# In a decoder layer with a selective scan, half of the scan's B·u products move from VectorE to ScalarE and GpSimd

## The chip, the cores and the metric

One core of a Trainium2 chip runs the whole kernel in one launch. The metric is the device time in microseconds, as the median of several runs. The engines are TensorE (PE), VectorE (DVE), ScalarE (ACT), GpSimd (POOL) and SyncE (SP). Each works through a row of instructions of its own, in order, and waits on semaphores for the others.

## The reference, cut to what matters

One decoder layer on 16 x 128 tokens of width 128: a selective state space block with a mixture of 4 experts, an attention, and a second mixture of 8 experts. The part that the change touches is the recurrence, per channel and for 16 states:

```python
def step(h, inps):
    x_t, d_t, B_t, C_t = inps
    bar_A = jnp.exp(jnp.minimum(d_t[:, :, None] * A, 2.0))
    bar_B = jnp.clip(d_t[:, :, None] * B_t[:, None, :], -2.0, 2.0)
    h = jnp.clip(bar_A * h + bar_B * x_t[:, :, None], -100.0, 100.0)
    y = jnp.sum(h * C_t[:, None, :], axis=-1) + x_t * D_param
    return (h, y)
```

The mixtures, the attention, the layer norms and their inputs all follow from y and are computed as before.

## The kernel before, in words

Channels lie on the 128 partitions, tokens along the free axis. The 16 sequences form four groups of four, 512 tokens each. A *unit* is one state of one group: k // 16 is the group, k % 16 the state, 64 units in all. For each unit

- ScalarE computes the decay a = exp(A·delta) in SBUF (`decay`, in batches of four, four to seven units ahead),
- TensorE broadcasts the row of B into a PSUM bank (`send_B`, banks 0 and 3 in turn) and the row of C into bank 1 (`send_C`),
- VectorE multiplies the B bank in place with u = delta·x (`drive`, L489), runs the scan h = a·h + drive (`scan`, L502), and multiplies h with C into hc (`read_out`, L537),
- GpSimd adds hc to the running output yD (`add_state`, L1072).

What sets the order is a loop over *slots* k that each engine's code runs through for itself; there is no other scheduler. In slot k VectorE issues scan(k), drive(k+1), read_out(k-1), then `around(k)`, the small work that is due in that slot. GpSimd's slot k is add_state(k-1) and then its share of the other work: in slots 5, 21 and 37 it splits rows into three bf16 parts, in others it adds a bias (L1020), forms delta (L1090), u (L1094) or a bound (L1098), or an inverse root. TensorE's slot k is send_B(k+2), its other work, send_C(k+1). The other work is the preparation of the next group, the first mixture of the group before and the attention of the one before that, all placed by slot number; from group 1 on it fills most of each engine's row. h is a ring of 3 units, hc of 3, a of 8. After slot 63 the tail begins: the last group's mixture and attention, the routing and the eight experts.

Every semaphore wait stands in the engine's own row, so all that is behind the waiting instruction waits too. `dve_done` counts VectorE's instructions, and `at[...]` holds the count of one of them.

Once for each group VectorE also bounds |h| (a scan of z, L468, both inputs in SBUF); where the bound is too large a slow clipped path runs, which these inputs do not take.

Of the kernel before, what the change touches and what calls it, by code (L numbers as in the profile page):

```python
# [5 lines left out]
ALU = mybir.AluOpType  # L6
# [143 lines left out]
def decoder_layer(nc, x, ctx, A_log, D_param, Wd, bd, WB, bB, WC, bC, Wr, br, up_w, up_b, down_w,  # L150
                  down_b, ln_w, ln_b, Wq, bq, Wk, bk, Wv, bv, wg, fc1_w, fc1_b, fc2_w, fc2_b,
                  ln_gamma, ln_beta, out):
    with ExitStack() as st:
# [39 lines left out]
            "p (e t d) -> p e t d", e=E2, t=FT)  # L193
        xe_early = sb("xe_early", [P, E2, ROW])
        xe_tok = sb("xe_tok", [P, 2, LT, ROW])
        xe_flat = w2[:].rearrange("p e t d -> p (e t d)")
        xeT = xe_flat[:, 0:2 * LATE].rearrange("p (b n) -> p b n", b=2)
        xeT_early = xe_flat[:, 2 * LATE:2 * LATE + LATE0]
# [113 lines left out]
        rows_ps, rows_done = sem("rows_ps"), sem("rows_done")  # L312
        bmax_ps, absx_done, amax_done = sem("bmax_ps"), sem("absx_done"), sem("amax_done")
        worst_ps = sem("worst_ps")
        a_done, B_ps, C_ps, y_started, summed = sem("a_done"), sem("B_ps"), sem("C_ps"), sem("y_started"), sem("summed")
        fcT_ps, fcT_done = sem("fcT_ps"), sem("fcT_done")
        ctxT_ps, ctxT_done = sem("ctxT_ps"), sem("ctxT_done")
# [45 lines left out]
            return ATT_BANK if g < G - 2 else C_BANK  # L363

        def drive_of(k):
            return bank[B_BANKS[k % 2]][:, 0:width(k // NS)]

        def state_of(k):
            return h[:, k % H_RING, 0:width(k // NS)]
# [12 lines left out]
        def _(v):  # L382
# [108 lines left out]

            def scan(k, clipped):

                v.wait_ge(dve_done, at["b", k])
                v.wait_ge(a_done, k + 1)
                if k >= H_RING:
                    v.wait_ge(dve_done, at["hc", k - H_RING])
                if clipped:
                    scan_clipped(k)
                    ins = v.tensor_scalar(state_of(k), state_of(k), CLIP_H, -CLIP_H, ALU.min, ALU.max)  # L500
                else:
                    ins = v.tensor_tensor_scan(state_of(k), decay_of(k).rearrange("p j n -> p (j n)"),  # L502
                                               drive_of(k), 0.0, ALU.mult, ALU.add)
                do(ins)
                at["h", k] = n[0]
# [283 lines left out]
            def slot(k, clipped=False):  # L789
                if 0 <= k < UNITS:  # L790
                    scan(k, clipped)
                if 0 <= k + 1 < UNITS and k >= 0:
                    drive(k + 1)
                if 1 <= k <= UNITS:
                    read_out(k - 1)
                around(k)
# [180 lines left out]
        def _(pool):  # L977
# [86 lines left out]
            def add_state(k):  # L1064
# [6 lines left out]
                pool.wait_ge(dve_done, at["hc", k])  # L1071
                pool.tensor_tensor(grp(yD, g), grp(yD, g), read_of(k), ALU.add).then_inc(summed, 1)  # L1072

            for k in range(FIRST_SLOT, LAST_SLOT + 1):
                if 0 <= k - 1 < UNITS:
                    add_state(k - 1)
                if k == PRE0:
                    inverse_root(quads(0), 0, 0)
                if k == PRE0 + 1:
                    inverse_root(slice(GT, TILES), 1, 0)  # L1080
                if (g := pre_at(k, 5)) is not None and g:
                    split_rows(g)
                if (g := pre_at(k, 13)) is not None:
                    pool.wait_ge(normed[0], g + 1)
                    pool.wait_ge(ld_affine, 16 * N_AFFINE)
                    add_bias(quads(g), 1)
                if (g := pre_at(k, 7)) is not None:
                    pool.wait_ge(sp_ln, g + 1)
                    pool.wait_ge(relu_done, g + 1)
                    pool.tensor_tensor(quad(delta, g), quad(delta, g), z1[:], ALU.add).then_inc(delta_done, 1)  # L1090
                if (g := pre_at(k, 8)) is not None:
                    pool.wait_ge(delta_done, g + 1)
                    pool.wait_ge(xT_done[0], g + 1)
                    pool.tensor_tensor(quad(u, g), quad(delta, g), quad(xT, g), ALU.mult).then_inc(u_done, 1)  # L1094
                if (g := pre_at(k, 11)) is not None:
                    pool.wait_ge(dve_done, at["boundmax", g])
                    pool.wait_ge(absx_done, g + 1)
                    pool.tensor_tensor(z2[:], z2[:], absx[:], ALU.mult).then_inc(w_done, 1)  # L1098
                if (g := att_at(k, 0)) is not None:
                    inverse_root(gsl(g), g, 1)  # L1100
                if (g := att_at(k, 3)) is not None:
                    inverse_root(gsl(g), g, 2)
                if (g := att_at(k, 5)) is not None:

                    pool.wait_ge(normed[2], g + 1)
                    add_bias(gsl(g), 4)
                if (g := att_at(k, 13)) is not None:
                    inverse_root(gsl(g), g, 3)
                if (g := att_at(k, 14)) is not None:

                    pool.wait_ge(normed[3], g + 1)
                    pool.tensor_copy(acc[:, gsl(g), :], xn[:, gsl(g), :]).then_inc(acc_done, 1)
                    pool.wait_ge(biased[4], g + 1)
                    add_bias(gsl(g), 3)
                for g, i in firsts_at(k):
                    if i == 0:
                        pool.wait_ge(zeroed, 16 * (QN + 2 * PG))
                    if i == START[G - 1]:
                        pool.wait_ge(scattered, 16 * 2 * START[G - 1])
                        pool.wait_ge(ld_early, 16)  # L1120
                    if i == counted(g).start:
                        pool.wait_ge(dve_done, at["pos", 0, g])
                    dispatch(0, i)
                    if i == TILES - 1:
                        pool.wait_ge(dve_done, at["pos", 1, g])
                        for second_of in tiles_of(g):
                            dispatch(1, second_of)
                if k in SECONDS_PARTS:
                    pool.wait_ge(dve_done, at["seconds"])
                    for i in SECONDS_PARTS[k]:  # L1130
                        dispatch(1, i)
# [23 lines left out]
        def _(act):  # L1155
# [40 lines left out]
            def silu(g, i):  # L1196
# [3 lines left out]
                if f == 0 and m >= 2:  # L1200
                    act.wait_ge(dn_ps, downs((m - 2) // E1, (m - 2) % E1 + 1))
                act.activation(hid[:, m % 2, f, 0:width(g)], bank[UP_BANKS[f % 2]][:, 0:width(g)], ACT.Silu,  # L1202
                               bias=cols[:, C_UPB + i:C_UPB + i + 1]).then_inc(hid_done, 1)

            for k in range(FIRST_SLOT, LAST_SLOT + 1):

                if (g := pre_at(k, 1)) is not None:
                    normalize(0, g, quads(g), xn, x_tok)
                if (g := att_at(k, 1)) is not None:
# [144 lines left out]
        def _(pe):  # L1354
# [19 lines left out]

            def send_B(k):
                if k >= 2:
                    pe.wait_ge(dve_done, at["h", k - 2])
                broadcast_row(B_BANKS[k % 2], k % NS, k // NS, B_ps)

            def send_C(k):  # L1380
# [191 lines left out]
            for k in range(FIRST_SLOT, LAST_SLOT + 1):  # L1572
                if k == 0:
                    send_B(0)
                    send_B(1)
                    send_C(0)
                if 0 <= k and k + 2 < UNITS:
                    send_B(k + 2)
                around(k)
                if k >= 0:  # L1580
                    next_up(k + 1)
                if 0 <= k and k + 1 < UNITS:
                    send_C(k + 1)
# [120 lines left out]
```

## Time and profile before

| | us |
|---|---|
| median of 3 runs | 481.47 (481.04 to 482.59) |
| profiled execution, its time | 482.02 |
| profiled execution, its span | 480.2 |
| TensorE busy | 344.7 (72%) |
| VectorE busy | 292.0 (61%) |
| ScalarE busy | 263.0 (55%) |
| GpSimd busy | 230.6 (48%) |
| granted TensorE clock, mean | 0.885 |

The shares are means over the whole span. The scan of the 64 units runs from 31 to 252 us, and the remaining 228 us hold the tail; the engines' shares differ between the two. A group of instructions in the profile has a line, an engine, an operation, its count, its busy time, the mean of one, and the idle time of the engine ahead of it with what ended it. Instructions of one engine overlap a little in the trace, so the pitch of their starts is shorter than their duration.

### The profile page before, as it was taken

What the parts mean: (1) busy time and instruction counts of PE and PEld (TensorE: products, weight loads), DVE (VectorE), ACT (ScalarE), POOL (GpSimd) and SP (SyncE); (2) the same over time, 40 slices, a digit from 0 to 9 for tenths busy, and PEclk for the clock granted to TensorE, in tenths of its full rate; (3) what the DMA queues carried; (4) which work ended last, traced back from release to release, by engine and by line L of the source; (5) the groups of instructions that cost most, each with busy time, mean ns of one, the idle gap of its engine ahead of it and who ended that gap; (6) DMA issues with size and microseconds to landing.
All of it is one profiled execution on the core that took longest, in us unless ns stands there. A gap on an engine that the chain in (4) does not pass through costs nothing. (4 is left out here: it accounts for less than half of the span.)

```text
span 480.2 us, 5947 instructions
## 1 busy us (share of the span) xinstructions
PE 344.7 (72%) x1749; PEld 233.6 (49%) x1749; DVE 292.0 (61%) x840; ACT 263.0 (55%) x465; POOL 230.6 (48%) x275
## 2 busy tenths in 40 slices
PE   1427557769896899978999688661537789999460
PEld 0203333346464565645667455561327757767360
DVE  3478988956999799999974245357136012222055
ACT  3554645668887797868537675413224474554021
POOL 4425755543545665464541422716844435455434
PEclk9999965879999899999899988975558899999966
DMA  6999400000000000000000000200120221210243
GB/s 123 290 233 333 124 1 1 0 0 1 1 1 0 2 1 1 1 2 0 1 1 2 0 0 9 81 1 23 50 61 28 77 67 49 76 53 14 78 120 88
DMA packets 29472, 23.94 MB, mean 50 GB/s; under 512 B 5448, under 2 KB 23943, under 8 KB 29440
## 3 DMA queue, kind: packets, MB, share of 16 engines
q1 hardware_dynamic: 27048, 19.50, 14.8%
q0 software_dynamic: 2304, 4.04, 2.5%
q8 instruction: 14, 0.23, 0.2%
q14 instruction: 18, 0.15, 0.1%
q10 hardware_dynamic: 88, 0.03, 0.0%
HBM read 13.73 MB, written 10.52 MB: 51 GB/s over the span
## 5 line engine op out<-in xcount | busy, mean ns | idle before, releaser
L1072 POOL TENSOR_TENSOR yD<-yD,hc 128x512 f32<-128x512 f32 x64 | 84.4, 1318 | 103.5 <-DVE hc L537 97.9
L1398 PE MATMUL bank<-yD,w 128*128 128x512 f32 x128 | 71.9, 645 | 17.1 <-ACT hid L1202 16.2
L502 DVE TENSOR_TENSOR_SCAN h<-a,bank 128x512 f32<-128x512 f32 x64 | 77.8, 1216 | 1.4 <-DVE bank L489 0.5
L1407 PE MATMUL bank<-w,hid 128*128 128x128 f32 x512 | 74.6, 293 | 0.0
L1407 PEld LDWEIGHTS bank<-w,hid 128*128 128x128 f32 x512 | 68.6, 205 | 9.4 <-issue 6.1
L1389 PE MATMUL bank<-rows,selid 99*128 99x512 bf16 x128 | 47.5, 457 | 25.5 <-DVE hc L537 23.4
L1135 POOL DMA_INDIRECT y_rows<-yslot,dest x40 | 39.1, 977 | 37.6 <-DVE yslot L865 22.1
L1202 ACT ACTIVATE hid<-bank,cols 128x512 f32<-128x512 f32 x64 | 43.4, 683 | 18.0 <-PE bank L1398 11.9
L489 DVE TENSOR_TENSOR bank<-bank,u 128x512 f32<-128x512 f32 x64 | 43.8, 684 | 14.5 <-PE bank L1389 14.2
L1060 POOL DMA_INDIRECT slots_in<-xrow,posu x32 | 32.3, 1010 | 32.7 <-DVE locs L684 14.7
L1389 PEld LDWEIGHTS bank<-rows,selid 99*128 99x128 bf16 x128 | 12.8, 106 | 67.4 <-DVE hc L537 47.0
L537 DVE TENSOR_TENSOR hc<-h,bank 128x512 f32<-128x512 f32 x64 | 43.3, 677 | 0.9 <-PE bank L1389 0.9
L1181 ACT ACTIVATE a<-delta,A_sb 128x508 f32<-128x508 f32 x64 | 40.5, 707 | 0.1
L865 DVE TENSOR_TENSOR yslot<-bank,w 128x128 f32<-128x128 f32 x32 | 9.2, 292 | 47.8 <-PE bank L1643 46.6
L593 DVE SCALAR_TENSOR_TENSOR acc<-bank,gate,acc 128x128 f32<-128x128 f32 x64 | 18.0, 344 | 29.5 <-PE bank L1407 29.4
L1338 ACT ACTIVATE hid<-bank,cols 128x512 f32<-128x512 f32 x32 | 22.0, 687 | 24.4 <-PE bank L1643 17.0
L1187 ACT ACTIVATE xrow<-x_tok,nmr,rstd 128x128 f32<-128x128 f32 x48 | 19.7, 482 | 23.2 <-POOL nmr L1037 23.2
L1372 PE MATMUL bank<-ident,xrow 128*128 128x128 f32 x48 | 9.5, 331 | 31.7 <-ACT xrow L1187 31.6
L1398 PEld LDWEIGHTS bank<-yD,w 128*128 128x128 f32 x128 | 20.8, 204 | 20.7 <-ACT hid L1202 18.1
L1643 PE MATMUL bank<-fc,hid 128*128 128x128 f32 x256 | 30.1, 275 | 0.7 <-DVE yslot L865 0.7
L1643 PEld LDWEIGHTS bank<-fc,hid 128*128 128x128 f32 x256 | 29.4, 192 | 1.8 <-issue 1.8
L1631 PE MATMUL bank<-w,fc1T 128*128 128x512 f32 x64 | 29.2, 596 | 1.5 <-ACT w L1320 1.5
(235 smaller groups left out, 586.4 us busy)
## 6 DMA issues: line engine op xcount, KB each, us to landing
slots_in<-yslot SPq DMA_DIRECT2D x10, 258.0 KB, 6.3
xe_tok<-slots_in SPq DMA_DIRECT2D x8, 258.0 KB
y_rows<-yslot SPq DMA_DIRECT2D x8, 256.0 KB, 5.2
x_tok<-in_x_dram SPq DMA_DIRECT2D x4, 256.0 KB, 3.9
w<-in_L_attn_up_w_dram SPq DMA_DIRECT2D x1, 1024.0 KB
yD<-y_rows SPq DMA_DIRECT2D x4, 256.0 KB, 4.4
xT<-y_rows SPq DMA_DIRECT2D x4, 256.0 KB, 5.7
out_dram<-acc SPq DMA_DIRECT2D x4, 256.0 KB, 2.3
```

Source lines behind the costliest of these rows:

```text
L489: do(v.tensor_tensor(drive_of(k), drive_of(k), grp(u, g), ALU.mult))
L502: ins = v.tensor_tensor_scan(state_of(k), decay_of(k).rearrange("p j n -> p (j n)"), drive_of(k), 0.0, ALU.mult, ALU.add)
L537: do(v.tensor_tensor(read_of(k), state_of(k), bank[C_BANK][:, 0:width(k // NS)], ALU.mult))
L1060: pool.indirect_dma_start(slots_in[:], bass.IndirectOffsetOnAxis(ap=posu[:, r, i:i + 1], axis=0), xrow[:, i, :], None, bounds_check=SLOTS - 1,
L1072: pool.tensor_tensor(grp(yD, g), grp(yD, g), read_of(k), ALU.add).then_inc(summed, 1)
L1135: pool.indirect_dma_start(y_rows[:], bass.IndirectOffsetOnAxis(ap=to, axis=0), yslot[:, half, j * P:(j + 1) * P], None, bounds_check=2 * T ...
L1181: act.activation(decay_of(k)[:, :, 1:P], tiles3(grp(delta, g))[:, :, 1:P], ACT.Exp, scale=A_sb[:, s:s + 1]).then_inc(a_done, 1)
L1202: act.activation(hid[:, m % 2, f, 0:width(g)], bank[UP_BANKS[f % 2]][:, 0:width(g)], ACT.Silu, bias=cols[:, C_UPB + i:C_UPB + i + 1]).then ...
L1389: pe.matmul(bank[b][:, 0:width(g)], selid[:, row:row + 1].to_broadcast([3 * NROW, P]), rows[:, p % 2, at_col:at_col + width(g)], start=Tru ...
L1398: pe.matmul(bank[UP_BANKS[f % 2]][:, 0:width(g)], w1[:, e, f * P:(f + 1) * P], grp(yD, g), start=True, stop=True).then_inc(up_ps, 1)
L1407: ins = pe.matmul(bank[DOWN_BANK][:, j * P:(j + 1) * P], hid[:, m % 2, f, j * P:(j + 1) * P], w2[:, e, f, :], start=(f == 0), stop=(f == F ...
L1643: ins = pe.matmul(bank[4 + t % 2][:, 0:P], hid2[:, e % 2, f, j * P:(j + 1) * P], fc2[:, e, f, :], start=(f == 0), stop=(f == FT - 1))
```

## The change

Even units keep what they had. For odd units ScalarE copies the broadcast B from PSUM bank 3 into `bu`, a ring of two units in SBUF (`copy_B`), and GpSimd multiplies it in place with u (`drive` on GpSimd). The scan of an odd unit reads `bu` in place of the bank. `bu` lies in the memory of `xe_tok`, which is loaded only in the tail. TensorE sends two B rows at the start of each even slot, and the odd one waits for ScalarE's copy instead of the scan.

```diff
@@ drive_of
-            return bank[B_BANKS[k % 2]][:, 0:width(k // NS)]
+            if k % 2:
+                return bu[:, k // 2 % 2, 0:width(k // NS)]
+            return bank[B_BANKS[0]][:, 0:width(k // NS)]
@@ VectorE, scan
-                v.wait_ge(dve_done, at["b", k])
+                if k % 2:
+                    v.wait_ge(bu_done, k // 2 + 1)
+                else:
+                    v.wait_ge(dve_done, at["b", k])
@@ VectorE, slot
-                if 0 <= k + 1 < UNITS and k >= 0:
+                if 0 <= k + 1 < UNITS and k >= 0 and k % 2:
                     drive(k + 1)
@@ GpSimd
+            def drive(k):
+
+                pool.wait_ge(b_copied, k // 2 + 1)
+                pool.wait_ge(u_done, pre_of(k // NS) + 1)
+                pool.tensor_tensor(drive_of(k), drive_of(k), grp(u, k // NS), ALU.mult).then_inc(bu_done, 1)
+
             for k in range(FIRST_SLOT, LAST_SLOT + 1):
+                if 0 <= k < UNITS and k % 2 == 0:
+                    drive(k + 1)
                 if 0 <= k - 1 < UNITS:
                     add_state(k - 1)
@@ ScalarE
+            def copy_B(k):
+
+                act.wait_ge(B_ps, k + 1)
+                if k >= 4:
+                    act.wait_ge(dve_done, at["h", k - 4])
+                act.activation(drive_of(k), bank[B_BANKS[1]][:, 0:width(k // NS)], ACT.Copy).then_inc(b_copied, 1)
+
             for k in range(FIRST_SLOT, LAST_SLOT + 1):
 
+                if k == 0:
+                    copy_B(1)
+                if k % 2 and 0 <= k and k + 2 < UNITS:
+                    copy_B(k + 2)
@@ TensorE, send_B and the loop
-                    pe.wait_ge(dve_done, at["h", k - 2])
+                    if k % 2:
+                        pe.wait_ge(b_copied, k // 2)
+                    else:
+                        pe.wait_ge(dve_done, at["h", k - 2])
...
-                if 0 <= k and k + 2 < UNITS:
+                if 0 <= k and k + 2 < UNITS and k % 2 == 0:
                     send_B(k + 2)
+                    send_B(k + 3)
```

GpSimd's row, from slot 6 on, before. L1072 is the sum of a unit, L1090 and L1094 form delta and u of the next group, L1098 the bound:

```order
L1072 TENSOR_TENSOR yD<-yD,hc 128x512 x2
L1090 TENSOR_TENSOR delta<-delta,z 128x512
L1072 TENSOR_TENSOR yD<-yD,hc 128x512
L1094 TENSOR_TENSOR u<-delta,xT 128x512
L1072 TENSOR_TENSOR yD<-yD,hc 128x512 x3
L1098 TENSOR_TENSOR z<-z 128x512
L1072 TENSOR_TENSOR yD<-yD,hc 128x512 x2
```

The same place after. L1085 is the new product (`bu` is named `xe_tok` here, after its memory), L1079 the sum, L1105, L1109 and L1113 are delta, u and the bound:

```order
L1085 TENSOR_TENSOR xe_tok<-xe_tok,u 128x512
L1079 TENSOR_TENSOR yD<-yD,hc 128x512 x2
L1105 TENSOR_TENSOR delta<-delta,z 128x512
L1085 TENSOR_TENSOR xe_tok<-xe_tok,u 128x512
L1079 TENSOR_TENSOR yD<-yD,hc 128x512
L1109 TENSOR_TENSOR u<-delta,xT 128x512
L1079 TENSOR_TENSOR yD<-yD,hc 128x512
L1085 TENSOR_TENSOR xe_tok<-xe_tok,u 128x512
L1079 TENSOR_TENSOR yD<-yD,hc 128x512 x2
L1113 TENSOR_TENSOR z<-z 128x512
```

The product of the odd unit k+1 stands at the head of even slot k, behind the sum of unit k-2 and the rest of slot k-1, ahead of the sum of unit k-1.

VectorE's row at the start of the scan, slots 0 to 3, before. A scan is listed as SCALAR_TENSOR_TENSOR:

```order
L502 SCALAR_TENSOR_TENSOR h<-a,bank 128x512
L489 TENSOR_TENSOR bank<-bank,u 128x512
L502 SCALAR_TENSOR_TENSOR h<-a,bank 128x512
L489 TENSOR_TENSOR bank<-bank,u 128x512
L537 TENSOR_TENSOR hc<-h,bank 128x512
L502 SCALAR_TENSOR_TENSOR h<-a,bank 128x512
L489 TENSOR_TENSOR bank<-bank,u 128x512
L537 TENSOR_TENSOR hc<-h,bank 128x512
L502 SCALAR_TENSOR_TENSOR h<-a,bank 128x512
```

The same slots after:

```order
L509 SCALAR_TENSOR_TENSOR h<-a,bank 128x512
L509 SCALAR_TENSOR_TENSOR h<-a,xe_tok 128x512
L493 TENSOR_TENSOR bank<-bank,u 128x512
L544 TENSOR_TENSOR hc<-h,bank 128x512
L509 SCALAR_TENSOR_TENSOR h<-a,bank 128x512
L544 TENSOR_TENSOR hc<-h,bank 128x512
L509 SCALAR_TENSOR_TENSOR h<-a,xe_tok 128x512
```

Every second product is gone from VectorE's row, and every second scan reads both inputs from SBUF.

## Rows read from the trace of the kernel before

**Rows 1.** Page, costliest groups: busy us, mean ns, idle before with releaser.

```profile
L1072 POOL TENSOR_TENSOR yD<-yD,hc 128x512 f32<-128x512 f32 x64 | 84.4, 1318 | 103.5 <-DVE hc L537 97.9
...
L502 DVE TENSOR_TENSOR_SCAN h<-a,bank 128x512 f32<-128x512 f32 x64 | 77.8, 1216 | 1.4 <-DVE bank L489 0.5
...
L489 DVE TENSOR_TENSOR bank<-bank,u 128x512 f32<-128x512 f32 x64 | 43.8, 684 | 14.5 <-PE bank L1389 14.2
...
L537 DVE TENSOR_TENSOR hc<-h,bank 128x512 f32<-128x512 f32 x64 | 43.3, 677 | 0.9 <-PE bank L1389 0.9
```

**Rows 2.** Windows: stretch, length, busy us and count of each engine, PE clock, DMA.

```profile
31.00:75.00 44.00, 25.49 (x81) 12.83 (x81) 41.11 (x56) 20.27 (x33) 25.07 (x23) 0.86 0.53 157
75.00:132.00 57.00, 45.33 (x187) 25.08 (x188) 45.40 (x85) 40.87 (x59) 27.69 (x25) 0.84 0.00 1
132.00:192.00 60.00, 52.72 (x278) 34.35 (x278) 54.85 (x114) 49.66 (x74) 33.23 (x35) 0.97 0.00 1
192.00:252.00 60.00, 53.76 (x287) 34.85 (x285) 55.27 (x134) 38.16 (x66) 29.93 (x32) 0.97 0.00 1
```

**Rows 3.** Waits from 96 to 252 us: total us, times, longest.

```profile
POOL yD L1072 <- DVE hc L537: 64.6, 34, 6.0
...
DVE bank L489 <- PE bank L1389: 12.1, 12, 4.9
```

**Rows 4.** Timeline of VectorE, slots 48 and 49: start us, duration us.

```profile
194.03 0.68 DVE L537 TENSOR_TENSOR hc<-h,bank 128x512 f32<-128x512 f32 x1
194.62 1.21 DVE L502 TENSOR_TENSOR_SCAN h<-a,bank 128x512 f32<-128x512 f32 x1
195.75 0.67 DVE L489 TENSOR_TENSOR bank<-bank,u 128x512 f32<-128x512 f32 x1
196.34 0.68 DVE L537 TENSOR_TENSOR hc<-h,bank 128x512 f32<-128x512 f32 x1
```

**Rows 5.** Timeline of GpSimd at five places.

```profile
48.73 0.30 POOL L1042 CAST parts<-bcm 128x132 bf16<-128x132 f32 x1
...
121.87 2.05 POOL L1072 TENSOR_TENSOR yD<-yD,hc 128x512 f32<-128x512 f32 x1 [0.42 <-DVE hc L537]
...
177.69 1.27 POOL L1098 TENSOR_TENSOR z<-z 128x512 f32<-128x512 f32 x1
178.92 1.27 POOL L1020 TENSOR_TENSOR x_tok<-x_tok,affine 128x512 f32<-128x512 f32 x1
180.14 2.19 POOL L1072 TENSOR_TENSOR yD<-yD,hc 128x512 f32<-128x512 f32 x1
...
194.85 1.27 POOL L1072 TENSOR_TENSOR yD<-yD,hc 128x512 f32<-128x512 f32 x1 [1.63 <-DVE hc L537]
...
209.41 0.20 POOL L1037 TENSOR_TENSOR nmr<-nmr,rstd 128x4 f32<-128x4 f32 x1
```

**Rows 6.** Timeline of VectorE: two instances of the z scan, both inputs in SBUF.

```profile
121.64 1.22 DVE L468 TENSOR_TENSOR_SCAN z<-am,z 128x512 f32<-128x512 f32 x1
...
179.15 2.12 DVE L468 TENSOR_TENSOR_SCAN z<-am,z 128x512 f32<-128x512 f32 x1
```

**Rows 7.** Groups of instructions: ScalarE's copies out of PSUM.

```profile
L1172 ACT ACTIVATE xT<-bank 128x512 f32<-128x512 f32 x12 | 7.1, 595 | 19.3 <-PE bank L1372 16.8 <-issue 2.5
```

**Rows 8.** Timeline of VectorE: C products that bound some pairs, and product 24.

```profile
44.56 0.68 DVE L537 TENSOR_TENSOR hc<-h,bank 128x512 f32<-128x512 f32 x1
...
51.09 0.68 DVE L537 TENSOR_TENSOR hc<-h,bank 128x512 f32<-128x512 f32 x1
...
102.55 0.70 DVE L489 TENSOR_TENSOR bank<-bank,u 128x512 f32<-128x512 f32 x1 [4.89 <-PE bank L1389]
...
204.34 0.68 DVE L537 TENSOR_TENSOR hc<-h,bank 128x512 f32<-128x512 f32 x1
...
211.71 0.68 DVE L537 TENSOR_TENSOR hc<-h,bank 128x512 f32<-128x512 f32 x1
...
237.44 0.68 DVE L537 TENSOR_TENSOR hc<-h,bank 128x512 f32<-128x512 f32 x1
```

**Rows 9.** Timeline of ScalarE, slots 20 and 21: a batch of decays, then silu.

```profile
93.06 2.53 ACT L1181 ACTIVATE a<-delta,A_sb 128x508 f32<-128x508 f32 x4
...
97.55 1.28 ACT L1202 ACT_TABLE_LOAD   x1
98.85 1.27 ACT L1202 ACTIVATE hid<-bank,cols 128x512 f32<-128x512 f32 x2
```

More of the change, by code:

```diff
@@ L195, in decoder_layer @@
         xe_tok = sb("xe_tok", [P, 2, LT, ROW])
+        bu = xe_tok[:].rearrange("p b j n -> p (b j n)")[:, 0:2 * GW].rearrange("p (r n) -> p r n", r=2)
         xe_flat = w2[:].rearrange("p e t d -> p (e t d)")
@@ L314, in decoder_layer @@
         worst_ps = sem("worst_ps")
+        b_copied, bu_done = sem("b_copied"), sem("bu_done")
         a_done, B_ps, C_ps, y_started, summed = sem("a_done"), sem("B_ps"), sem("C_ps"), sem("y_started"), sem("summed")
```

## The prediction

> **What bounds the kernel now.** I read the page's groups first. The scan over 64 units takes four large operations a unit: VectorE's scan (1,216 ns), its product B·u (684), its product with C (677), and GpSimd's sum into yD (1,318) [rows 1]. Then the windows: VectorE is busy 41.11 of 44 us in the first group of units, 54.85 of 60 in the third, 55.27 of 60 in the fourth; in the second, 45.40 of 57, TensorE and ScalarE hold it up [rows 2]. Then the waits of 96 to 252 us: GpSimd waits 64.6 us for VectorE's C product, so it is the slack engine; VectorE waits 12.1 us for the broadcasts [rows 3]. So VectorE's in-order row sets the scan's pace, 31 to 252 us. In the timeline of a slot without other work its instructions start 0.59 us (C product to scan), 1.13 (scan to B product) and 0.59 (B product to C product) apart, 2.31 us a slot [rows 4]. What follows 252 us is not touched and starts when the scan ends.
>
> **What is removed.** 32 products leave VectorE's row, one per pair of slots (even k, odd k+1). One is worth its pitch, 0.59 us, not its 684 ns: 32 x 0.59 = 18.9 us if nothing takes their place [rows 4].
>
> **What is added on ScalarE.** 32 copies of 512 columns from PSUM; the nearest row, the same form, is 595 ns: 19 us in a row that is busy 149 of the 221 us from 31 to 252 [rows 2, 7]. No table load stands ahead of such a copy in the trace. The copy for unit k+2 stands at the head of ScalarE's slot k, more than a slot before it is needed, so I cost it at nothing where ScalarE keeps up. The cover is gone where an exponential batch and table loads stand ahead of it, in slots 5, 21 and 37; in slot 21 it ends near 100.1 us (the silu pair ahead starts at 98.85) [rows 9], counted below.
>
> **What is added on GpSimd, and where.** 32 products of 128x512. GpSimd's own two-input products and sums last 1.27 us and follow each other by 1.23 to 1.24 [rows 5]. In its row drive(k+1) stands behind add(k-2) and whatever GpSimd does in slot k-1, and ahead of add(k-1). Take time 0 as the start of the C product of unit k-2. By the rows the scan of unit k starts at 0.59, add(k-2) at 0.82 [rows 4, 5]. Without the product the C product of k-1 starts at 1.72, and VectorE wants to scan unit k+1 at 2.31. But GpSimd starts drive(k+1) at 0.82 + 1.23 = 2.05 and ends it at 3.3. This is the first stall, at least 1.0 us, because add(k-2) cannot start earlier than it does today.
>
> **The second stall.** The scan before reads decay in SBUF and drive in PSUM, and its 64 instances take 1,216 ns in the mean; the one at 194.62 took 1.21 us although a sum of GpSimd started at 194.85 [rows 1, 4, 5]. The odd scans will read both from SBUF. The trace has a scan of that form, of z: 1.22 us where it starts before GpSimd's sum, which then lasts 2.05 instead of 1.27; 2.12 us where a GpSimd sum began 0.23 us ahead of it [rows 5, 6]. They exclude each other for a whole instruction. In the new order GpSimd ends drive(k+1) and goes straight on to add(k-1), whose input has long been there, at 3.28; VectorE still needs the semaphore, about 0.2 us. So the sum goes first, until 4.55, and the scan behind it ends 1.08 us after that, as the z scan did (181.27 against 180.19) [rows 5, 6]: 5.63. The unit k product starts 0.08 before that end, the C product of unit k 0.58 later: 6.13 us a pair. Before it was 4.60 at the faster pitch, 4.82 in the first group.
>
> The Trainium skill (SBUF — State Buffer, "Who interferes with whom") says the same as a rule that speaks against this change: a VectorE instruction with two SBUF inputs contends with a GpSimd instruction that reads SBUF, with one SBUF input it does not, and whoever issues first holds the shared ports for the whole instruction. The trace agrees, 2.12 against 1.22 us. By this rule the pair takes 6.13 us; without it 5.1.
>
> **The sum, pair by pair**, each as new minus old distance between the C products of units k-2 and k; the old ones are differences of rows like those of [rows 4, 8]:
> - Bare pairs (k = 2, 4, 10, 16, 32, 36, 48): 6.13 against 4.82, 4.82, 5.86, 4.83, 5.01, 5.03 and 5.22, the longer ones holding a wait for TensorE or a small operation: +7.3 us.
> - One more GpSimd operation of the slot before stands ahead of drive: 7.36 us. k = 8, 14, 30, 46, 60 had 4.82, 5.21, 6.49, 7.02 and 5.25 (from 237.44 on) [rows 8]: +8.0. k = 12, 28, 44, where VectorE's z scan is also held: +0.9 each, 2.7. k = 40: +0.8. k = 24 and 26 together +0.5, since VectorE waited for TensorE there.
> - Five small operations split the rows ahead of drive (k = 6, 22, 38). At k = 6 they end at 49.03, 4.47 after time 0; drive, sum and scan make it 8.55 against 6.53 [rows 5, 8]: +2.0. At k = 22 ScalarE's copy ends near 100.1, product, sum and scan put the next product at 103.7 against 102.55 [rows 8, 9]: +1.15, which also swallows k = 20. k = 38: +1.7. Together 4.9.
> - The inverse root ahead of drive (k = 42, 52, 58). At k = 52 it ends at 209.61, 5.27 after time 0, and the pair takes 9.4 against 7.37 [rows 5, 8]: +2.0; the two others +0.7 each: 3.4.
> - Where VectorE has 1.6 us or more of other work in the even slot, or the first pair, both stalls hide (k = 0, 18, 34, 50, 54, 56, 62): -4.5.
>
> Together 7.3 + 8.0 + 2.7 + 0.8 + 0.5 + 4.9 + 3.4 - 4.5 = +23.1 us. Only 4.5 of the 18.9 us are gained, in the covered pairs. I give a later scan end to the total one to one: TensorE and ScalarE work off their rest from 252 us on in the order they have now. The profiled execution has a span of 480.2 and a time of 482.02 us; 482.02 + 23.1 = 505.1, and the median of the runs lies 0.55 under it: **504.6 us**.
>
> **PSUM and TensorE.** The broadcast of an odd B now waits only for ScalarE's copy and goes out a slot earlier. It is one instruction earlier in TensorE's row, ahead of the slot's other work; cost nothing, and some of VectorE's 12.1 us of waits [rows 3] go, at most the share counted above.
>
> **Rivals.**
> - *No exclusion between odd scan and sum* (the drive in PSUM was not what spared the scan). Then only the queue position counts: the pair 5.1 us, about 1.0 less in bare pairs and in those with one more operation, 20 pairs, so 505 - 20 = 485. Against: the 2.12 us row. Chance 0.1.
> - *The stalls hide, the change gains.* This needs GpSimd to be done with drive(k+1) when VectorE asks. It is so wherever VectorE is itself held long in both slots. If it were general, 18.9 less about 5 for pairs that TensorE sets (VectorE's 12.1 us of waits, part of them kept): 468. For it: GpSimd is idle 64.6 us in that stage. Against: that idle time lies before add(k-2), drive stands after it. Chance 0.05.
> - *ScalarE becomes the bound*, slower than forecast. It has 49.66 of 60 us busy from 132 to 192 [rows 2]; 8 copies make it 54.4. Each copy is now in a chain TensorE - ScalarE - GpSimd - VectorE, and silu, which feeds TensorE, is queued behind it. If eight of the places behind an exponential batch (2.53 us, and 1.28 for a table load) [rows 9] cost 1.5 us more each, 505 + 12 = 517. It decides when ScalarE's idle time in a slot is under 0.6 us. Chance 0.2, as slower slots also give it room.
> - *Nothing changes*: gains and stalls cancel, as the first rival with more cover would have it, near 481. Chance 0.03.
> - The forecast, give or take 8 us: 0.62.
>
> **Range and chances.** Low 488 (the first rival's upper edge; pairs I took as stalled may be covered), high 518 (the third). About 0.3% is what a measurement of this kernel tells from no change. Faster 0.05, same 0.03, slower 0.92.
>
> **What would show it.** In the changed trace: odd scans of 2.0 to 2.3 us, even ones 1.21; GpSimd's product at 1.27 us, followed at once by the sum; bare pairs of 6.1 us; VectorE's idle time ahead of odd scans released by GpSimd's product, 1 us or more each, some 25 to 35 us in all; copies near 600 ns; the scan's end at about 275 instead of 252 us, and the same 228 us behind it. Wrong, if odd scans take 1.2 us under a running sum, if the copy, not the product's place in the row, is what the odd scan waits for, or if TensorE's granted clock, 0.97 in the last two groups [rows 2], falls with the slower pace.

## The result and the profile after

| | before | changed |
|---|---|---|
| median us | 482.03 (4 runs, 481.04 to 484.96) | 504.03 (4 runs, 502.88 to 507.83) |
| ratio | | 1.046, 95% interval 1.0387 to 1.0533 |
| profiled execution, span us | 480.2 | 501.1 |
| last C product of the scan starts | 251.27 | 277.37 |
| granted TensorE clock, mean | 0.885 | 0.848 |

The change costs 22.0 us, 4.6%. The page's groups of the changed kernel, which answer to [rows 1]; the scans are from the groups kept apart by form. The columns are busy us, mean ns of one, and idle us before with its releaser:

```profile
L1079 POOL TENSOR_TENSOR yD<-yD,hc 128x512 f32<-128x512 f32 x64 | 83.7, 1308 | 72.6 <-DVE hc L544 69.2
L509 DVE TENSOR_TENSOR_SCAN h<-a,xe_tok 128x512 f32<-128x512 f32 x32 | 60.4, 1889 | 25.4 <-POOL xe_tok L1085 23.5
L1085 POOL TENSOR_TENSOR xe_tok<-xe_tok,u 128x512 f32<-128x512 f32 x32 | 42.0, 1311 | 13.4 <-ACT xe_tok L1225 13.1
L544 DVE TENSOR_TENSOR hc<-h,bank 128x512 f32<-128x512 f32 x64 | 42.7, 668 | 1.6 <-DVE h L509 1.0
L509 DVE TENSOR_TENSOR_SCAN h<-a,bank 128x512 f32<-128x512 f32 x32 | 38.8, 1212 | 0.5 <-DVE bank L493 0.4
```

The even scans last 1,212 ns as before, the odd ones 1,889 in the mean: 20 of the 32 lasted 2.17 to 2.29 us, most others 1.20 to 1.23. VectorE was idle 25.4 us ahead of the odd ones, 23.5 of it until GpSimd's product. 32 x (1,889 - 1,212) ns is 21.7 us in longer scans. Together that is 47 us of loss on VectorE. From 31 us to the last C product its waits for the experts' matmuls also grew, from 3.9 to 12.3 us, and the four z scans took 2.1 us more. Against this stand the removed products, 18.9 us by their pitch (43.8 us busy in [rows 1], 21.5 now), and the waits of the B product for its broadcast, 14.2 us before and 0.7 now. The balance is some 25 us, and the last C product came 26.1 us later.

The two stalls are seen in one bare pair. VectorE, slots 32 and 33 (start us, duration us):

```profile
143.68 0.67 DVE L544 TENSOR_TENSOR hc<-h,bank 128x512 f32<-128x512 f32 x1
144.27 1.21 DVE L509 TENSOR_TENSOR_SCAN h<-a,bank 128x512 f32<-128x512 f32 x1
145.40 0.66 DVE L544 TENSOR_TENSOR hc<-h,bank 128x512 f32<-128x512 f32 x1
147.02 2.29 DVE L509 TENSOR_TENSOR_SCAN h<-a,xe_tok 128x512 f32<-128x512 f32 x1 [0.97 <-POOL xe_tok L1085]
149.23 0.67 DVE L493 TENSOR_TENSOR bank<-bank,u 128x512 f32<-128x512 f32 x1
149.81 0.67 DVE L544 TENSOR_TENSOR hc<-h,bank 128x512 f32<-128x512 f32 x1
```

and GpSimd beside it:

```profile
144.49 1.27 POOL L1079 TENSOR_TENSOR yD<-yD,hc 128x512 f32<-128x512 f32 x1 [2.40 <-DVE hc L544]
145.72 1.27 POOL L1085 TENSOR_TENSOR xe_tok<-xe_tok,u 128x512 f32<-128x512 f32 x1
146.95 1.28 POOL L1079 TENSOR_TENSOR yD<-yD,hc 128x512 f32<-128x512 f32 x1
150.63 1.27 POOL L1079 TENSOR_TENSOR yD<-yD,hc 128x512 f32<-128x512 f32 x1 [2.40 <-DVE hc L544]
```

GpSimd's product cannot start before the sum of unit 30 is through (145.72) and ends at 146.99. VectorE, free since 146.06, starts its scan at 147.02, but the sum of unit 31 had started at 146.95 and holds the scan until 148.2, so that it takes 2.29 us. From C product to C product the pair is 6.13 us, where it was 5.01, or 4.60 where nothing waited.

### The profile page after: what moved, and what is told of

The parts are those of the page before. It is cut to its first block, busy times and chain, and to the rows that moved or that the text cites. A ratio compares the mean times of both kernels' runs of the same rounds, so it can differ in the third digit from the quotient of the medians.

```text
span 501.1 us, 6009 instructions
## 1 busy us (share of the span) xinstructions
PE 356.2 (71%) x1749; PEld 239.9 (48%) x1749; DVE 298.2 (60%) x808; ACT 279.2 (56%) x497; POOL 274.3 (55%) x307
## 4 chain that ended last, share of the span: by engine, by line
PE 38%; DVE 17%; issue 16%; POOL 15%; ACT 9%; DMA 3%; another core or an unknown queue 2%; DVEq 1%; SPq 0%; POOLq 0%; ACTq 0%
PE bank L1436 7%; PE bank L1673 6%; PE bank L1661 6%; PE bank L1427 5%; POOL xe_tok L1085 4%; DVE bank L493 3%; DVE hc L544 3%; POOL yD L1079 3%; PE bank L1418 2%; POOL rstd L1040 2%; POOL slots_in L1067 2%; DVE acc L600 2%; PE bank L1519 2%; DVE z L472 1%
## 5 line engine op out<-in xcount | busy, mean ns | idle before, releaser
L1079 POOL TENSOR_TENSOR yD<-yD,hc 128x512 f32<-128x512 f32 x64 | 83.7, 1308 | 72.6 <-DVE hc L544 69.2
L1427 PE MATMUL bank<-yD,w 128*128 128x512 f32 x128 | 76.2, 680 | 11.9 <-ACT hid L1217 10.9
L1418 PE MATMUL bank<-rows,selid 99*128 99x512 bf16 x128 | 50.3, 482 | 43.0 <-DVE hc L544 40.9
L1436 PE MATMUL bank<-w,hid 128*128 128x128 f32 x512 | 77.2, 300 | 0.4 <-DVE lg L626 0.4
L1436 PEld LDWEIGHTS bank<-w,hid 128*128 128x128 f32 x512 | 71.4, 212 | 9.7 <-issue 6.3
L509 DVE TENSOR_TENSOR_SCAN h<-a,xe_tok 128x512 f32<-128x512 f32 x32 | 60.4, 1889 | 25.4 <-POOL xe_tok L1085 23.5
L1085 POOL TENSOR_TENSOR xe_tok<-xe_tok,u 128x512 f32<-128x512 f32 x32 | 42.0, 1311 | 13.4 <-ACT xe_tok L1225 13.1
L509 DVE TENSOR_TENSOR_SCAN h<-a,bank 128x512 f32<-128x512 f32 x32 | 38.8, 1212 | 0.5 <-DVE bank L493 0.4
L1364 ACT ACTIVATE hid<-bank,cols 128x512 f32<-128x512 f32 x32 | 22.0, 687 | 24.4 <-PE bank L1673 14.2
L1036 POOL TENSOR_SCALAR vpe<-mv 128x4 f32<-128x4 f32 (+1 forms) x18 | 6.9, 383 | 50.0 <-DVE mv L403 47.2
L1398 PE MATMUL bank<-ident,xrow 128*128 128x128 f32 x48 | 10.9, 371 | 30.2 <-ACT xrow L1202 30.2
L1661 PE MATMUL bank<-w,fc1T 128*128 128x512 f32 x64 | 29.2, 596 | 1.6 <-ACT w L1346 1.6
```

The source lines that it names most:

```text
L1085: pool.tensor_tensor(drive_of(k), drive_of(k), grp(u, k // NS), ALU.mult).then_inc(bu_done, 1)
L1418: pe.matmul(bank[b][:, 0:width(g)], selid[:, row:row + 1].to_broadcast([3 * NROW, P]), rows[:, p % 2, at_col:at_col + width(g)], start=Tru ...
L1427: pe.matmul(bank[UP_BANKS[f % 2]][:, 0:width(g)], w1[:, e, f * P:(f + 1) * P], grp(yD, g), start=True, stop=True).then_inc(up_ps, 1)
L1436: ins = pe.matmul(bank[DOWN_BANK][:, j * P:(j + 1) * P], hid[:, m % 2, f, j * P:(j + 1) * P], w2[:, e, f, :], start=(f == 0), stop=(f == F ...
L1661: pe.matmul(bank[m % 4][:], fc1T[:, e, f * P:(f + 1) * P], xeT[:, e % 2, :], start=True, stop=True).then_inc(up2_ps, 1)
```

## The experiments

Every kernel was timed beside the kernel before on the same chip. That kernel's time ranged from 474.4 to 485.0 us over the chips and runs, so effects are given by ratios; 1% is 4.8 us. An effect that is the difference of two ratios carries both intervals. The last column is from one profiled execution of each kernel; in those of e6 and e8 the first scan started 2 us earlier than in the others (29.1 and 29.2 us against 31.1 to 31.2), in a part that no edit touches.

| kernel | ratio to before | 95% interval | last C product, us |
|---|---|---|---|
| changed | 1.046 | 1.0387 to 1.0533 | 277.37 |
| e1, GpSimd's product one slot earlier | 1.0624 | 1.0561 to 1.0688 | 284.42 |
| e2, odd scan reads PSUM bank 3 | 1.0685 | 1.0609 to 1.076 | 287.52 |
| e3, kernel before, odd product into SBUF | 1.0077 | 1.0017 to 1.0137 | 255.3 |
| e4, changed, no product on GpSimd | 1.007 | 1.0004 to 1.0135 | 253.46 |
| e5, odd scan with one SBUF input | 1.0202 | 1.0104 to 1.0301 | 262.92 |
| e6, kernel before, no odd products | 0.9909 | 0.9867 to 0.995 | 243.49 |
| e7, changed, sum behind the odd scan | 1.0307 | 1.0224 to 1.0391 | 268.57 |
| e8, five covered units alone | 1.0181 | 1.0108 to 1.0254 | 258.3 |
| e9, e6 with ScalarE's copies beside it | 0.9908 | 0.9872 to 0.9943 | 249.27 |

**Is it the exclusion?** Four kernels. First the exclusion without anything else: VectorE keeps all its products and writes the odd ones into SBUF.

```diff
-                do(v.tensor_tensor(drive_of(k), drive_of(k), grp(u, g), ALU.mult))
+                do(v.tensor_tensor(drive_of(k), bank[B_BANKS[k % 2]][:, 0:width(g)], grp(u, g), ALU.mult))
```

> The kernel before, with one change: VectorE writes the product of odd units to SBUF in place of PSUM, so that odd scans read both inputs from SBUF, with no copy and no product elsewhere. Theory (the exclusion costs VectorE only where GpSimd's operation starts first): bare pairs stay at 4.60 to 4.82 us, odd scans there 1.22 and the sums beside them about 2.05; in a few covered pairs the scan is held; whole 482 to 487 us. Rival (a scan with both inputs in SBUF costs a microsecond more everywhere under a running sum): 32 us more, near 510.

Measured 484.47 us, ratio 1.0077. Its scans by form:

```profile
L505 DVE TENSOR_TENSOR_SCAN h<-a,xe_tok 128x512 f32<-128x512 f32 x32 | 42.1, 1315 | 0.7 <-DVE flags L484 0.4
L505 DVE TENSOR_TENSOR_SCAN h<-a,bank 128x512 f32<-128x512 f32 x32 | 38.8, 1213 | 0.7 <-DVE bank L492 0.4
```

Two SBUF inputs by themselves cost next to nothing: 25 of the 32 odd scans lasted 1.21 to 1.23 us. The mean of 1,315 ns comes from seven others, above all the scans of units 15 and 41 at 2.13 and 2.18 us. The bare pairs are as before (4.83 us for pair 2, 5.01 for pair 32). In this order the scan starts ahead of the sum, and the sum waits (1,489 ns in the mean against 1,318). The exclusion is cheap, 0.8% here, as long as VectorE comes first.

Next, the changed kernel with the odd scan reading something in PSUM after it has waited for GpSimd's product. The first version read bank 3:

```diff
-                                               drive_of(k), 0.0, ALU.mult, ALU.add)
+                                               (bank[B_BANKS[1]][:, 0:width(k // NS)] if k % 2 else drive_of(k)), 0.0, ALU.mult, ALU.add)
...
                         pe.wait_ge(b_copied, k // 2)
+                        pe.wait_ge(dve_done, at["h", k - 2])
```

> The changed kernel, but an odd scan waits for GpSimd's product as before and then reads the unmultiplied B from PSUM bank 3 (so the factor u is left out of the odd units' drive). Everything else, all three operations of GpSimd and their order, stays. Theory (two stalls): odd scans last 1.21 us in place of 2.27, the wait for the product stays near 1 us, bare pairs 5.1 us; whole near 484 us, 479 to 490. Rival (the queue position alone, odd scans being slow for another reason such as reading the drive from SBUF): odd scans stay at 2.27 and the whole at 504, or scans become short and the wait longer by as much.

Measured 514.16 us where 479 to 490 was expected, slower still, and no answer as a whole: the scan reads the bank, so TensorE's next odd B has to wait for the scan, and as that B stands at the head of the even slot, all of TensorE's slot waits behind it. Only the first group of units, where TensorE has little to do, shows the scan by itself: pairs 2, 8 and 14 fell from 6.12, 7.34 and 7.34 us to 5.06, 6.29 and 6.35, odd scans to 1.22, as the two stalls say. The second version reads the C bank, which keeps TensorE's waits:

```diff
-                                               drive_of(k), 0.0, ALU.mult, ALU.add)
+                                               (bank[C_BANK][:, 0:width(k // NS)] if k % 2 else drive_of(k)), 0.0, ALU.mult, ALU.add)
...
                     v.wait_ge(bu_done, k // 2 + 1)
+                    v.wait_ge(C_ps, k)
```

> The changed kernel, but an odd scan waits for GpSimd's product and then reads its second input from the C bank in PSUM, where the row of the unit before lies at that time (the odd drive is left out). Unlike the kernel that read bank 3, TensorE's waits stay those of the changed kernel. Theory (exclusion is the second stall): every odd scan 1.21 us, bare pairs 5.1 us against 6.12, pairs with one more GpSimd operation 6.3 against 7.34, in all four groups; whole 504 less about 15 to 20, 484 to 489. Rival (the exclusion only moves the wait): odd scans short, but pairs stay at 6.1 and the whole near 504.

Measured 490.89 us, ratio 1.0202, against 1.046. VectorE and then GpSimd at slots 32 and 33 of this kernel:

```profile
138.98 1.21 DVE L510 TENSOR_TENSOR_SCAN h<-a,bank 128x512 f32<-128x512 f32 x1
140.11 0.66 DVE L545 TENSOR_TENSOR hc<-h,bank 128x512 f32<-128x512 f32 x1
141.75 1.22 DVE L510 TENSOR_TENSOR_SCAN h<-a,bank 128x512 f32<-128x512 f32 x1 [0.97 <-POOL xe_tok L1086]
```

```profile
140.44 1.27 POOL L1086 TENSOR_TENSOR xe_tok<-xe_tok,u 128x512 f32<-128x512 f32 x1
141.66 1.28 POOL L1080 TENSOR_TENSOR yD<-yD,hc 128x512 f32<-128x512 f32 x1
```

The wait for the product is the same 0.97 us, and the sum starts ahead of the scan as in the changed kernel, but a scan with one SBUF input runs beside it in 1.22 us. The pair is 5.08 us against 6.13. So the second stall is the exclusion, some 2.6% of the whole, 12 us; with the two intervals it can be 1 to 4%. In the traces the last C product came 14.5 us earlier. This kernel's added wait for the C row held three odd scans for 4.8 us in all, so the exclusion may cost more than the 12 us. The time lies just above the 484 to 489 us expected.

A kernel that leaves nothing out says the same from the other side: GpSimd's sum waits until the scan is through.

```diff
                 pool.wait_ge(dve_done, at["hc", k])
+                if k % 2 and k + 2 < UNITS:
+                    pool.wait_ge(dve_done, at["h", k + 2])
```

> The changed kernel with one more wait: GpSimd's sum of an odd-numbered unit waits until the next odd scan is done, so that the scan never finds the shared port taken by it. Nothing is left out. In the slots counted from even k this is add(k-1) behind scan(k+1). Theory (the sum that starts ahead costs VectorE about 1.05 us in some 20 pairs): odd scans 1.22 us, bare pairs 5.1 to 5.3 us, whole 486 to 492. Rival (GpSimd then becomes the bound, its three operations and the excluded scan adding up to 4.9 us a pair and the delayed sum holding up the next product): bare pairs near 6 us, whole unchanged or longer.

Measured 494.4 us, ratio 1.0307, a little above the range given. Its scans and their waits:

```profile
L509 DVE TENSOR_TENSOR_SCAN h<-a,xe_tok 128x512 f32<-128x512 f32 x32 | 39.1, 1223 | 31.1 <-POOL xe_tok L1087 28.6
```

All odd scans are at 1,223 ns, six of the seven bare pairs at 5.07 to 5.29 us; pair 10 took 6.39. It wins 1.5% of the 4.6. In the pairs with other VectorE work it gives some back: pairs 34 and 40 grew to 9.54 and 11.73 us, from 7.28 and 9.09. In pair 34 VectorE waited 2.08 us for the experts' matmuls, 0.56 in the changed kernel. In pair 40 it waited 1.41 us for ScalarE and 2.23 us for a broadcast, 0.49 and 0.39 in the changed kernel. Why TensorE and ScalarE were later there is open.

**Is it the product's place in GpSimd's row?** The same product one slot earlier, ahead of a sum for which GpSimd now waits idle:

```diff
-                if 0 <= k < UNITS and k % 2 == 0:
-                    drive(k + 1)
+                if k == 0:
+                    drive(1)
+                if k % 2 and 0 <= k and k + 2 < UNITS:
+                    drive(k + 2)
```

> The same work as the changed kernel; only GpSimd's product for unit k+2 stands one slot earlier in its row, at the head of odd slot k ahead of add(k-1), in time in which GpSimd now waits for the C product. Theory (the place in GpSimd's row costs the time, by a stall for the product and then by the sum holding the port that the odd scan needs): bare pairs fall from 6.13 to 4.0 to 4.2 us, odd scans last 1.22 us, GpSimd's sums beside them about 2.1; the whole near 472 us, 466 to 480, since TensorE's waits come back. Rival (the exclusion costs wherever the product stands): odd scans stay near 2.2 us, bare pairs 5 us or more, whole 490 or more. Rival (ScalarE's copies are late once the pace rises): GpSimd's product waits for the copy in most pairs, whole 480 to 495.

Measured 511.03 us, slower than the changed kernel, and my main expectation (472 us) failed by 39 us. Parts of both rivals came true, though the time lies above the second one's 480 to 495 us. Waits from 31 to 255 us, with us in total, times, and longest:

```profile
POOL xe_tok L1085 <- ACT xe_tok L1227: 49.5, 15, 7.8
...
DVE h L509 <- POOL xe_tok L1085: 14.7, 9, 4.6
```

The odd B goes out at the head of even slot k and ScalarE copies it at the head of slot k+1, the very slot in which GpSimd now wants it. In 15 pairs it was not there, and GpSimd waited up to 7.8 us for it; at the old place the product came a slot later, and such waits came to 13.1 us. With the product late again, the next sum still went ahead of the odd scan, so both stalls were still there (busy us, mean ns, idle us before):

```profile
L509 DVE TENSOR_TENSOR_SCAN h<-a,xe_tok 128x512 f32<-128x512 f32 x32 | 58.0, 1811 | 23.2 <-POOL xe_tok L1085 18.2
```

That is little less than the 1,889 ns and 25.4 us of the changed kernel. So this run shows that moving the product alone does not help. A kernel in which the odd B, its copy and the product all come a slot earlier was not run.

There is also a floor that I had not set up in the forecast. It is an estimate. An odd scan excludes GpSimd, so in each pair two sums, a product and an odd scan must come one after the other: 3 x 1.23 + 1.13 = 4.8 us [rows 4, 5]. A single pair can be shorter where GpSimd carries a sum over into the next one, as pair 2 of this kernel, 4.27 us, which pair 4 followed at 5.77. The shortest pairs of the kernel before take 4.61 to 4.83 us. So by this sum even the best place would not shorten many pairs in a row.

**What is the product on GpSimd worth in all?**

```diff
-                pool.tensor_tensor(drive_of(k), drive_of(k), grp(u, k // NS), ALU.mult).then_inc(bu_done, 1)
...
-                    v.wait_ge(bu_done, k // 2 + 1)
+                    v.wait_ge(b_copied, k // 2 + 1)
```

> The changed kernel without GpSimd's product: odd scans wait for ScalarE's copy and read the unmultiplied B from it (the factor u is left out of the odd units' drive). What is left of the change are ScalarE's 32 copies, TensorE's earlier odd B, and VectorE's 32 products gone. Theory (copies cost nothing, the product's place costs all): bare pairs 4.0 to 4.1 us, whole 468 to 474 us, TensorE taking back some 5 of the 18.9 us. Rival (ScalarE's copies are a good part of the loss): the whole at 480 or above, with waits of VectorE for the copy beyond slots 5, 21 and 37.

Measured 484.19 us, ratio 1.007. So the product costs 3.9% of the whole, 19 us. If e5 is the measure, 12 of them are the exclusion and the rest the wait for the product; that split is by subtraction only, and the exclusion is not all gone here, as the odd scans still last 1,374 ns in the mean. But the first theory said 468 to 474, and the run stood on the rival's side. With 18.9 us of products gone from VectorE the kernel is no faster than before. Two more kernels ask where these went.

**What are the removed products worth?** The kernel before without its odd products, and nothing in their place:

```diff
-                do(v.tensor_tensor(drive_of(k), drive_of(k), grp(u, g), ALU.mult))
+                if k % 2 == 0:
+                    do(v.tensor_tensor(drive_of(k), drive_of(k), grp(u, g), ALU.mult))
...
+                if k % 2:
+                    v.wait_ge(B_ps, k + 1)
```

> The kernel before with the odd units' product left out and nothing in its place (the odd scan reads the unmultiplied B from its bank). It shows what the removed 32 products are worth by themselves. Theory A (VectorE sets the scan's pace): 18.9 us less on VectorE, TensorE takes back 5, whole 468. Theory B (TensorE and ScalarE stand close behind VectorE, as the run without GpSimd's product at 484 suggests): whole 472 to 479, with waits of VectorE for the broadcasts and for the experts' matmuls grown by 8 us or more. The difference to the run without GpSimd's product (484.2) is then the price of ScalarE's copies and their place in the chain.

Measured 474.78 us, ratio 0.9909: 4.4 us are won (2.4 to 6.4 by the interval), not 18.9 and not the 13.9 that I had left over (theory B). VectorE's longest waits from 31 to 260 us, of the kernel before and then of this one:

```profile
DVE bank L489 <- PE bank L1389: 14.2, 14, 4.9
DVE acc L593 <- PE bank L1407: 10.8, 7, 6.9
```

```profile
DVE acc L597 <- PE bank L1411: 16.1, 9, 6.9
DVE bank L490 <- PE bank L1393: 15.4, 9, 5.3
```

The waits for TensorE grew from 25.0 to 31.5 us. The last C product came 7.8 us earlier (243.49 against 251.27), but 2.1 of these lie ahead of the first scan; between the first scan and the last C product 5.7 us are won. Of the seven bare pairs only 2, 16 and 48 win the pitch, 4.12 us for 4.83, 4.12 for 4.82 and 4.61 for 5.22. Pairs 4, 32 and 36 stay (4.93, 4.98 and 5.03 against 4.97, 5.01 and 5.03), as VectorE then waits 0.5 to 0.9 us for the next broadcast, and pair 10 grows from 5.86 to 6.14, with 2.02 us of such a wait. Pairs with other work, such as 26, 34, 46, 50 and 54, win nothing either (8.55, 7.69, 7.03, 8.04, 9.41); in the first four VectorE waits 1.0 to 2.0 us for the experts' matmuls. And in pairs 12 and 28 the earlier VectorE meets GpSimd: its z scan, both inputs in SBUF, is now held, and they take 8.30 us for 7.57 and 7.56.

**And the copies?** ScalarE copies 512 columns of u at the same places, and nobody waits for them:

```diff
+            def copy_u(k):
+                act.wait_ge(u_done, pre_of(k // NS) + 1)
...
+                act.activation(bu[:, k // 2 % 2, 0:width(k // NS)], grp(u, k // NS), ACT.Copy).then_inc(b_copied, 1)
```

> The kernel before with the odd products left out (474.8 us by itself), and ScalarE's 32 copies at their places in its row, but copying 512 columns of u, and with nobody waiting for them. The run without GpSimd's product took 484.2 us; it has the same copies, and TensorE, ScalarE and VectorE wait on each other through them. Theory A (the copies' 19 us in ScalarE's row cost, since silu and the decays stand behind them): 480 to 484 us. Theory B (their place in the chain costs: a late copy holds the odd scan and lets GpSimd's sum take the port first): 474 to 478 us.

Measured 476.73 us, ratio 0.9908, the same as without them. The 32 copies are there, 19.9 us of ScalarE's time:

```profile
L1215 ACT ACTIVATE xe_tok<-u 128x512 f32<-128x512 f32 x32 | 19.9, 622 | 0.0
```

So the copies' time in ScalarE's row has no effect that these runs can tell; the two intervals leave room for some 3 us either way. What is left between this kernel and e4 is 1.6%, 8 us (0.9908 to 1.007). The two differ in three things: in e4 the copies are waited for, TensorE sends the odd B in another order, and the odd scan reads both inputs from SBUF, which makes it 160 ns longer in the mean, 5 us in all. Theory B named the first and the third together; how the 8 us divide is not shown. In the two profiled executions the stretch from first scan to last C product differs by 4.2 us, with pairs 6, 40, 54 and 56 longer in e4 by 1.0 to 2.3 us each and others shorter.

How a wait and the exclusion add up is seen in e4 at pair 10, VectorE:

```profile
56.50 0.66 DVE L545 TENSOR_TENSOR hc<-h,bank 128x512 f32<-128x512 f32 x1
57.97 2.24 DVE L510 TENSOR_TENSOR_SCAN h<-a,xe_tok 128x512 f32<-128x512 f32 x1 [0.82 <-ACT xe_tok L1223]
```

The copy comes 0.82 us late, and by then a sum of GpSimd is running: the scan takes 1.0 us more. The lateness is doubled. This pair is no longer for it than in e9 (5.95 us against 6.14), where VectorE waits 2.02 us for a broadcast instead; pair 6 is (7.36 against 5.09). The copy was waited for in pairs 6, 10, 22 and 38, for 1.86, 0.82, 3.97 and 1.63 us.

**A version that uses only what is covered.** The forecast said that pairs with much other VectorE work gain. Five units, with TensorE's order as before, and the copy at the end of ScalarE's slot, since the B for it goes out a slot later:

```diff
+MOVED = (19, 27, 35, 51, 63)
...
+                if k + 2 in MOVED:
+                    copy_B(k + 2)
```

> Copy and GpSimd product for five units alone, 19, 27, 35, 51 and 63, whose pairs have other VectorE work of 1.6 us or more in the even slot; all others as in the kernel before, TensorE's order too. Theory (in covered pairs both stalls hide): each of these pairs 0.3 to 0.6 us shorter than in the kernel before, odd scans there 1.22 us, whole 479 to 482, so faster than before by 0 to 0.6%. Rival (the lower pace of VectorE in these pairs was TensorE's, so nothing is gained): the whole 481.5 to 483.

Measured 488.0 us, ratio 1.0181: slower by 1.8%, where I expected up to 0.6% faster, and outside the rival too. GpSimd's product in this kernel, and VectorE at unit 27:

```profile
L1086 POOL TENSOR_TENSOR xe_tok<-xe_tok,u 128x512 f32<-128x512 f32 x5 | 6.4, 1272 | 17.1 <-ACT xe_tok L1226 17.1
```

```profile
116.23 2.27 DVE L510 TENSOR_TENSOR_SCAN h<-a,xe_tok 128x512 f32<-128x512 f32 x1 [1.49 <-POOL xe_tok L1086]
```

At the end of the slot the copy stands behind silu and all the rest, and GpSimd waited 17.1 us for five of them. The pairs of the five units took 7.91, 11.20, 9.95, 9.84 and 9.04 us, where they had taken 7.64, 8.55, 7.57, 8.00 and 6.40. It is not shown that these units would gain with the early copy. But e6, which has no product at all for them, took 7.63, 8.55, 7.69, 8.04 and 6.40 us there: with TensorE's order as before, VectorE's product is worth nothing in these pairs. No version tried that does all the work beats the kernel before.

## Why the prediction was right, point by point

The forecast of 504.6 us met 504.03. It is right in direction, mechanism and most terms; part of the closeness is luck. In the profiled executions the change is +20.9 us where +23.1 was forecast: the scan was put 3.4 us too short and the rest of the kernel 5.2 us too long. Within the scan, too, errors cancel, +2.7 and +2.9 against -1.9 and -0.9. Its terms against the pairs' lengths, read between C products as in the prediction:

| term | forecast | measured |
|---|---|---|
| bare pairs (2, 4, 10, 16, 32, 36, 48) | +7.3 | +7.1 |
| one more GpSimd operation (8, 14, 30, 46, 60) | +8.0 | +8.3 |
| with the z scan (12, 28, 44) | +2.7 | +2.9 |
| pair 40 | +0.8 | +1.2 |
| pairs 24 and 26 | +0.5 | -0.4 |
| split rows (6, 20 with 22, 38) | +4.9 | +3.0 |
| inverse root (42, 52, 58) | +3.4 | +6.1 |
| covered (0, 18, 34, 50, 54, 56, 62) | -4.5 | -1.6 |
| sum, at the C product of unit 62 | +23.1 | +26.5 |
| the last slot | 0 | -0.4 |
| the rest of the kernel | 0 | -5.2 |

The prediction took pair 4 of the kernel before at 4.82 us; it was 4.97 (39.59 to 44.56). Most of the excess in the row of the inverse root comes from pair 58, forecast at +0.7 us and measured at +3.1.

- **The first stall**, the product's place behind add(k-2): 1.0 us forecast; VectorE was idle 0.95 to 0.97 us in six of the seven bare pairs. In pair 48 it was 0.36, as a reduction stands in its row there. Right. Its share of the whole is not measured by itself.
- **The second stall**, the exclusion, from a single row of 2.12 us: odd scans 2.27 to 2.29, bare pairs 6.11 to 6.13 against 6.13. Right, shown by e5 and e7. The idle time ahead of odd scans was put at some 25 to 35 us; it was 25.4 us, and the loss by the exclusion stands inside the longer scans.
- **No exclusion**, the first rival, 485: e5 is that case made, at a ratio of 1.0202, 490.9 us. Its price of 20 us was too high; it was about 12.
- **Copies at nothing**: right for their time (e9), too low for the chain: in the changed kernel GpSimd waited 13.1 us for copies, in six pairs. The cover named for slots 5, 21 and 37 did fail there, and in e4 also in slot 9.
- **18.9 us of removed products**: the wrong term. I had most of it consumed by the stalls and so it did little harm to the sum, but the second rival's 468 rests on it. By e6, which only leaves the products out, about 475 was the least that the move could give with TensorE's order as it was.
- **Covered pairs**: forecast too large. Pair 18 gained 1.1 and pair 62 0.9, but 54 and 56 lost 0.9 each. In pair 54 VectorE waited 2.02 us for the experts' matmuls; the granted clock was 0.64 in that pair, 1.00 in the kernel before. In pair 56 two small routing operations with two SBUF inputs were held, the first by GpSimd's sum, the second by its product, which started at 244.78:

```profile
244.15 0.72 DVE L558 TENSOR_TENSOR dif<-lg,mx 128x32 f32<-128x32 f32 x1
244.79 1.28 DVE L559 TENSOR_TENSOR dif<-mx 128x8 f32<-128x8 f32 x1
```

- **TensorE's clock**, named as what would make it wrong, did fall: from 0.97 in the last two groups [rows 2] to 0.92 from 147 to 213 us and 0.81 from 213 to 275. Pair 58 took 10.66 us against 7.51. Windows around it (busy us and count of PE, PEld, DVE, ACT, POOL, then the granted clock):

```profile
242.00:250.00 8.00, 6.64 (x39) 4.37 (x39) 7.86 (x22) 7.49 (x14) 5.48 (x6) 0.98 0.01 2
250.00:262.00 12.00, 12.00 (x35) 7.80 (x35) 7.92 (x19) 5.46 (x10) 5.39 (x7) 0.50 0.00 0
262.00:275.00 13.00, 13.00 (x68) 8.29 (x66) 10.25 (x14) 5.26 (x9) 8.68 (x7) 0.95 0.01 1
```

  TensorE was granted half speed, 1.2 GHz, from 250 to 262 us, and eight matmuls of an expert took 2.08 us. At the same place in the kernel before they took 1.61, and 1.06 where the full 2.4 GHz were granted. VectorE waited 3.78 us for them:

```profile
257.43 2.08 PE L1436 MATMUL bank<-w,hid 128*128 128x128 f32 x8
259.54 1.13 DVE L600 SCALAR_TENSOR_TENSOR acc<-bank,gate,acc 128x128 f32<-128x128 f32 x4 [3.78 <-PE bank L1436]
```

  TensorE was busy 6.64 of 8 us before that; in the kernel before pairs 56 and 58 ran at 1.00 and 0.77. Whether the slower pace brought the clock down is open. Other kernels that were slower than the kernel before, e1, e5 and e7, were granted 1.00 in pair 58, and it took them 7.00 to 7.29 us; e2 was granted 0.84, and it took 10.58.
- **One to one into the total**: wrong by 5.2 us. The last C product came 26.1 us later, the load of the early experts' tokens 23.3 later (378.63 against 355.33), the last loads 22.6 later (476.81 against 454.26), the end 20.9. In the other kernels the stretch from the last C product to the end is 224.9 to 227.8 us, against 228.9 before and 223.7 here, each from one execution, and executions of the kernel before alone differ by some 10 us. The gain comes in small steps. One of them is the clock: of TensorE's last 48 matmuls the first 32 took 6.46 us before and 5.27 here. Two of them started every 0.43 us where half speed was granted (0.51 before, 0.50 here) and every 0.22 where it was 1.00, and the half speed ended 5.6 us after the first before, 3.1 us here. The other steps stay open.

## What to carry to other kernels

Idle time of an engine is not a place for work until the row order is read: what matters is when the new instruction can start in its engine's row, and what queues behind it. An operand that moves from PSUM to SBUF can turn a VectorE instruction into one that excludes GpSimd, so count each pair's VectorE instructions with two SBUF inputs and GpSimd's instructions that read SBUF as one serial sum (4.8 us here); if that reaches the present pace (4.6 to 4.8 us), expect no gain. Before pricing a removed instruction at its pitch, leave it out in a run: here 18.9 us of VectorE's time were worth 4.4. And look at the pairs one by one: the gain was whole in some and nothing in others, where the next wait took its place.

## What the runs showed of the hardware that was not expected

- Being first decides by little. The odd scan lost to a sum that had started 0.07 us ahead of it (146.95 against 147.02) and took 2.29 us; where the sum started 0.23 us later than a scan of z, in the kernel before, the scan took 1.22 us and the sum 2.05 [rows 5, 6].
- A small instruction is held as long as a large one: the 128x8 subtraction took 1.28 us beside GpSimd's product, to the product's end, and 0.16 us in the kernel before. The trace shows this wait as the instruction's own duration, with no idle time ahead of it.
- ScalarE took 32 more activations, 19.9 us, in a stage where it was busy 149 of 221 us, with no measurable effect on the whole (0.9908 against 0.9909). The kernel that waits for such copies and reads them from SBUF took 8 us more.
